# Two groups' inverse deviations at once, and rows normalised four steps behind at the head of ScalarE's step

## The reference

```python
x = _layernorm(x + _L0_gnn_ref(x, ...))   # attention over the edges, 4 heads of 16, then a gate:
    # beta = sigmoid(concat([out, x_r, out - x_r]) @ W_beta)
    # out = beta * x_r + (1.0 - beta) * out;  return out @ W_m2n
x = _layernorm(x + _L1_gnn_ref(x, ...))   # relu(X @ w1 + segment_sum((X @ w2)[src] * ew, dst) + b)

def _layernorm(x, axis=-1, eps=1e-05):
    m = jnp.mean(x, axis=axis, keepdims=True)
    v = jnp.var(x, axis=axis, keepdims=True)
    return (x - m) / jnp.sqrt(v + eps)
```

## Time and profile before

| | |
|---|---|
| median of 3 runs | 1889.04 us (1883.46 to 1889.10) |
| profiled execution | 1893.35 us, its span 1891.7 us |
| edge-and-dense stage | 53 to 711 us of the span |
| scans | 711 to 811.5 us |
| correction, second layer, rows with edges | 811.5 to 1891.7 us |

### The profile page before, as it was taken

One profiled execution on the slowest core, in us unless ns is written; L12 is line 12 of the kernel. 1 busy time (PEld: TensorE's weight loads), 2 busy tenths in 40 slices (PEclk: granted clock), 3 DMA queues, 4 the chain that ended last, 5 costly groups with the idle time before them and its releaser, 6 DMA issues.

```text
span 1891.7 us, 35753 instructions
## 1 busy us (share of the span) xinstructions
PE 1232.4 (65%) x8398; PEld 1070.5 (57%) x8398; DVE 1334.5 (71%) x4876; ACT 1227.0 (65%) x4224; POOL 1061.7 (56%) x1183
## 2 busy tenths in 40 slices
PE   0677777776776760077888887777767766665553
PEld 0666666666666650056766665666656655565552
DVE  2677777777777769977777676888888865545453
ACT  0688888888888890047787776888888862222221
POOL 0555555555555531025555555788878856655565
PEclk9999999999999995589999999999999987777886
DMA  5688888888888879114444444988888842222221
GB/s 167 206 285 293 286 276 280 293 287 280 283 289 290 280 246 302 42 49 146 136 148 132 131 147 134 290 255 256 256 248 260 261 139 74 75 73 73 74 73 40
DMA packets 210063, 371.55 MB, mean 196 GB/s; under 512 B 36724, under 2 KB 67805, under 8 KB 208919
## 3 DMA queue, kind: packets, MB, share of 16 engines
q1 hardware_dynamic: 120822, 200.52, 33.7%
q10 hardware_dynamic: 57739, 108.12, 15.4%
q0 software_dynamic: 31360, 61.17, 13.1%
HBM read 231.39 MB, written 161.37 MB: 208 GB/s over the span
## 4 chain that ended last, share of the span: by engine, by line
PE 24%; issue 21%; POOL 16%; DVE 11%; ACT 10%; another core or an unknown queue 7%; DMA 6%; SPq 4%; ACTq 1%; DVEq 0%; POOLq 0%
POOL ring_a L487 11%; PE pd L552 5%; POOL big L493 4%; PE pk L531 3%; DMA scan_buf<-in_xT 3%; PE pd L583 2%; PE pd L582 2%; DVE val L1043 2%; ACT scan_buf L705 1%; PE pk L652 1%; PE pd L549 1%; ACT hout L705 1%; SPq L322 1%; DMA ew_t<-in_ew 1%
## 5 line engine op out<-in xcount | busy, mean ns | idle before, releaser
L946 DVE BATCH_NORM_STATS2 stats<-hpre 128x6 f32<-128x256 f32 x882 | 334.1, 420 | 0.1
L450 POOL DMA_INDIRECT ring_a<-in_x,gidx x196 | 185.5, 946 | 256.0 <-PE pt L543 208.7
L705 ACT ACTIVATE scan_buf<-hpre,nb,rs 128x128 f32<-128x128 f32 x686 | 292.1, 480 | 22.0 <-issue 13.1
L705 ACT ACTIVATE hout<-hpre,nb,rs 128x128 f32<-128x128 f32 x686 | 292.4, 481 | 20.0 <-issue 12.6
L472 POOL DMA_INDIRECT h_tab<-alpha,sidx x148 | 151.2, 1021 | 214.8 <-ACT alpha L776 169.4
L487 POOL DMA_INDIRECT ring_a<-h_tab,gidx x196 | 209.7, 1070 | 60.1 <-POOL big L493 52.3
L984 DVE SCALAR_TENSOR_TENSOR hpre<-pd,beta,xg 128x128 f32<-128x128 f32 x784 | 220.8, 345 | 25.3
L552 PE MATMUL pd<-w_sx,scan_buf 128*128 128x129 f32 x1568 | 232.8, 278 | 0.0
L531 PE MATMUL pk<-b_kvq,pair 128*128 128x192 f32 x392 | 117.2, 381 | 172.8 <-issue 161.2
L453 POOL DMA_INDIRECT ring_b<-in_x,gidx x196 | 185.4, 946 | 60.5 <-issue 60.5
L552 PEld LDWEIGHTS pd<-w_sx,scan_buf 128*128 128x128 f32 x1568 | 210.6, 194 | 4.8
(11 more groups left out here) (188 smaller groups left out, 3458.3 us busy)
## 6 DMA issues: line engine op xcount, KB each, us to landing
xg<-in_x SPq DMA_DIRECT2D x196, 256.0 KB
scan_buf<-in_xT SPq DMA_DIRECT2D x196, 256.0 KB
val<-h_tab SPq DMA_DIRECT2D x139, 256.0 KB
h_tab<-hout ACTq DMA_DIRECT2D x98, 256.0 KB
h_tab<-scan_buf ACTq DMA_DIRECT2D x98, 256.0 KB
out_z<-hout ACTq DMA_DIRECT2D x98, 256.0 KB
out_z<-scan_buf ACTq DMA_DIRECT2D x98, 256.0 KB
h_two<-h_tab SPq DMA_DIRECT2D x57, 256.0 KB, 8.9
```

Of the source, the lines that this page charges most:

```text
L450: gp.indirect_dma_start(out=ring_a[:, u, :], out_offset=None, in_=x[:, :], in_offset=bass.IndirectOffsetOnAxis(ap=gidx[:, k, 0:1], axis=0))\
L705: ins = act.activation(hout[ju][:, i * D:(i + 1) * D], hpre[:, ju, i * D:(i + 1) * D], ACT.Identity, bias=nb_of(ju, i), scale=rs_of(ju, i))
L946: ins = dve.bn_stats(stats[:, ju, i, :, :].rearrange("p j s -> p (j s)"), two)
```

## The change

Three things change, all in the edge-and-dense stage. ScalarE makes Ln and Exp for two groups at once, in even steps only, for groups k-2 and k-1, behind the gate's Exp. VectorE makes the negated means of two groups at once, in odd steps only, for groups k-3 and k-2, behind its `hpre` instructions. ScalarE normalises all four rows of group k-4 (not k-3) at the head of its step, ahead of the `val` copy. The store of group k-4 stays at the step's end. VectorE's program has one more step at the end.

```diff
--- before.py
+++ after.py
@@ -161,6 +161,9 @@
         def nb_of(ju, i):
             return nb[:, ju, i // 2, i % 2:i % 2 + 1]
 
+        def spread_of(ju, n):
+            return stats[:, ju:ju + n, :, :, :].rearrange("p u a b s -> p (u a b) s")[:, :, 2]
+
         def mean_of(ju, i):
             return stats[:, ju, i // 2, i % 2, 1:2]
 
@@ -709,6 +712,11 @@
             act.wait_ge(S["z_cp"], 16)
 
             def step_a(k, u, it):
+                if live(k, 4, T):
+                    g, gu, itg = back(k, u, it, 4)
+                    wait(act, S["nb_d1"], g + 1)
+                    wait(act, ring["h_st"][gu], 16 * itg)
+                    scale_rows(gu, NJ).then_inc(S["na_d1"], 1)
                 if live(k, 1, T):
                     j, ju, _ = back(k, u, it, 1)
                     wait(act, S["kv_a"], j + 1)
@@ -727,20 +735,15 @@
                     wait(act, S["mm_d1"], k + 1)
                     wait(act, S["pre_d1"], k - 1)
                     exp_minus(act, em[:, u % 2, :], pd[:, u % 2, :, D], S["cl_d1"], S["em_d1"], k)
-                if live(k, 3, T):
-                    g, gu, itg = back(k, u, it, 3)
-                    wait(act, S["nb_d1"], g + 1)
-                    wait(act, ring["h_st"][gu], 16 * itg)
-                    scale_rows(gu, NJ - 1)
-                if live(k, 1, T):
-                    wait(act, S["bn_d1"], j + 1)
-                    act.activation(lv[:, ju, :, :], stats[:, ju, :, :, 2], ACT.Ln, bias=eps_c[:, 0:1], scale=1.0 / D)\
-                        .then_inc(S["lv_d1"], 1)
-                if live(k, 3, T):
-                    scale_rows(gu, NJ, NJ - 1).then_inc(S["na_d1"], 1)
-                if live(k, 1, T):
-                    wait(act, S["lv_d1"], j + 1)
-                    act.activation(rs[:, ju, :, :], lv[:, ju, :, :], ACT.Exp, scale=-0.5).then_inc(S["rs_d1"], 1)
+                if u % 2 == 0 and live(k, 2, T):
+                    g, gu, _ = back(k, u, it, 2)
+                    wait(act, S["bn_d1"], g + 2)
+                    act.activation(lv[:, gu:gu + 2, :, :].rearrange("p u a b -> p (u a b)"), spread_of(gu, 2), ACT.Ln,
+                                   bias=eps_c[:, 0:1], scale=1.0 / D).then_inc(S["lv_d1"], 2)
+                    wait(act, S["lv_d1"], g + 2)
+                    act.activation(rs[:, gu:gu + 2, :, :].rearrange("p u a b -> p (u a b)"),
+                                   lv[:, gu:gu + 2, :, :].rearrange("p u a b -> p (u a b)"), ACT.Exp, scale=-0.5)\
+                        .then_inc(S["rs_d1"], 2)
                 if live(k, 4, T):
                     g, gu, _ = back(k, u, it, 4)
                     wait(act, S["na_d1"], g + 1)
@@ -986,14 +989,18 @@
                             scalar=beta[:, u % 2, i:i + 1], in1=xg[:, u, i * D:(i + 1) * D],
                             op0=ALU.mult, op1=ALU.add)
                     ins.then_inc(S["pre_d1"], 1)
-                if live(k, 2, T):
-                    g, gu, _ = back(k, u, it, 2)
-                    wait(dve, S["rs_d1"], g + 1)
-                    neg_mean(gu, NJ // 2).then_inc(S["nb_d1"], 1)
+                if u % 2 == 1 and live(k, 3, T):
+                    g, gu, _ = back(k, u, it, 3)
+                    wait(dve, S["rs_d1"], g + 2)
+                    dve.scalar_tensor_tensor(
+                        out=nb[:, gu:gu + 2, :, :].rearrange("p u a b -> p (u a b)"),
+                        in0=stats[:, gu:gu + 2, :, :, :].rearrange("p u a b s -> p (u a b) s")[:, :, 1], scalar=-1.0,
+                        in1=rs[:, gu:gu + 2, :, :].rearrange("p u a b -> p (u a b)"),
+                        op0=ALU.mult, op1=ALU.mult).then_inc(S["nb_d1"], 2)
                 if live(k, 0, T):
                     wait(dve, S["pre_d1"], k + 1)
                     pair_stats(u, NJ // 2).then_inc(S["bn_d1"], 1)
-            run_steps(dve, T, 2, step_a)
+            run_steps(dve, T, 3, step_a)
 
 
             dve.wait_ge(S["v_a"], T)
```

## The result

The changed kernel takes 2024.08 us (median of 4 runs, 2021.16 to 2024.39) against 1886.25 us for the kernel before (median of 4, 1882.74 to 1889.10): ratio 1.0726, 95% interval 1.0702 to 1.0750. It is 138 us slower.

A forecast was written before the change was run, and what follows sets the result against it. ScalarE, its instructions and issue time, was taken to bound the stage. A four-step loop of 3.66 + 4.50 + 3.57 + 4.50 = 16.23 us against 13.13 gave about +144 us, so 2033 us, range 2010 to 2075.

The forecast's parts named there:

- Exp to the first row, odd to even: ScalarE's even-step rows wait for VectorE's negated mean from the step before, starting 2.12 us after the gate's Exp starts.
- Four rows: ScalarE's four row instructions at the step's head take 4 x 0.385 = 1.54 us, to the next start.
- `val` to Exp: On ScalarE, from the `val` copy's start to the gate's Exp: 0.84 us, as in a quiet step before.
- Exp to the first row, even to odd: On ScalarE, grouped Ln and Exp, then the store's issue: rows start 1.19 us after the gate's Exp starts.
- 8 numbers cost nothing more than 4: Grouped Ln and Exp on ScalarE handle 8 numbers per partition instead of 4, costing at most 0.01 us more.
- The extra 0.09 us at u = 0: The step after u = 0 stays 0.09 us longer, as before: 3.66 us from Exp to Exp instead of 3.57.
- The drain: One more step at the stage's end adds 2 us: four rows of 1.54 and an issue.
- The waits on loads: 7.5 us of the stage's 647.6 are waits on loads, which a slower loop should mostly absorb; +7 if they stay.
- Rival 1: TensorE's clock falls in its longer idle gaps, Relu of odd steps waits 0.7 us: 2101, or 2067 in half; chance 0.18.
- 1.08 us of cover: TensorE's product ends at 2.20 us after Exp's start; Relu of an odd step asks at 3.28, so it is covered.
- rival 2: Negated mean is there in time and grouping pays: -0.52 us a loop, -25 us, 1864 us; chance 0.04.
- rival 3: The wait is met but the store's issue is bared: 13.72 us a loop, +29 us, 1918; chance 0.04.

The follow-up runs named there:

- second run: The changed kernel run again without edit, in the group of runs where the kernel before takes about 1760 us: 1897.56 us against 1760.06, ratio 1.0779.
- the one with the rows back: Changed kernel with the four rows, still four behind, moved back behind the gate's Exp, ahead of the grouped Ln and Exp: 1824.69 us against 1759.14, ratio 1.0373.
- kernel before with the store moved: Kernel before with the store moved from the step's end to between the `big` copy and Relu: 1723.09 us against 1760.06, ratio 0.9782.
- kernel with the longer wait: Changed kernel with the two groups' negated means made behind the two stats instructions of VectorE's odd step: 1997.59 us against 1759.14, ratio 1.1348.
- kernel with the negated means first: Changed kernel with the two groups' negated means made at the head of VectorE's odd step, ahead of `ep`: 1766.5 us against 1759.14, ratio 1.0040.
- all three together: Changed kernel with negated means ahead of `ep` and the store between `big` and Relu: ratio 0.9800 in one group of runs, 1.0153 in the other.

## Why the prediction was right

**Direction and mechanism.** Forecast 2033 us with 2010 to 2075, measured 2024. The wait came where it was placed: ahead of the rows of even steps, on the negated mean of the step before. Removing it alone takes back 130 of 137.5 us; making it 0.79 us longer costs the 77 us that this predicts, and 24 more in the other steps. The cause is shown, not only argued. The second run's trace names `nb` as what ended the wait in 75 even steps, 1.9 us on average.

**The sum.** Forecast 16.23 us in a loop, measured 15.94; the forecast's +144 became +131 in the span. Its terms:

- Exp to the first row, odd to even: 2.12 forecast; 2.20 (u = 3) and 2.10 (u = 1: 408.33 to 410.43) measured. The negated mean ends 1.77 us behind the Exp, for 1.78 forecast, and the release took 0.13 us at u = 3 where the forecast had 0.04.
- Four rows: 1.54 forecast, 1.55 measured.
- `val` to Exp: 0.84 taken from the earlier trace rows, 0.76 measured (404.06 to 404.82). Four times 0.08 is about the 0.3 us that the loop is shorter; the other errors of this list, +0.12 and -0.09, nearly cancel. This is the term of the sum that was mis-sized. In the kernel before `val`, `q_sb` and `big` start 0.12 and 0.15 us apart, here 0.10 and 0.11. So the spacing was not the instructions' own, as I had taken it to be, and the runs show what it hangs on. `val` to Exp is 0.84 us in the kernels where `val` starts idle, 0.18 us behind the end of the store's issue (both traces of the kernel before, and the one with the rows back). It is 0.76 in those where rows run ahead of `val` and the store stays at the step's end. In the kernel before with the store moved, `val`, `q_sb` and `big` start 0.10 us apart too. The store ahead of `val` was what spread them; why it does is not shown.
- Exp to the first row, even to odd: 1.19 forecast, 1.20 measured, but by luck, since two errors cancel. The store is issued at E + 0.76 and not at E + 0.67, mostly because Exp starts 0.38 behind the Ln of 8 numbers instead of 0.31; and the rows start 0.10 behind the issue's end instead of 0.18. The forecast that 8 numbers cost nothing more than 4 was short by these 0.07 us; the durations of the instructions (0.29 for 0.28) don't show it. The grouped Ln also counts its semaphore up by two and not by one, and no run separates that from the 8 numbers.
- The extra 0.09 us at u = 0: not there (3.51 and 3.50).
- The drain: from the last Exp to the scans 12.8 us instead of 10.3, forecast 2 more.

**The waits on loads** were forecast to be mostly absorbed; the slowest step from odd to even is 4.54 us and only one from even to odd reached 4.0, so they were.

**Rival 1, the clock.** Half right. The granted clock over the stage fell to 0.93 from the 0.98 of the earlier trace rows: between 60 and 830 us it fell to the lower level 32 times, for 3.4 us each, so in about one pair of steps in three. But this stayed hidden, and only just:

```profile
406.88 1.07 PE L555 MATMUL pd<-w_sx,scan_buf 128*128 128x129 f32 x4
...
408.04 0.26 ACT L669 ACTIVATE em<-pd,top_c 128x4 f32<-128x4 f32 x1
```

The rival had TensorE's work at the lower clock throughout, 4.1 us, and Relu 0.7 us late. In the loop the clock fell only ahead of the products: the work from 404.69 to 407.95 took 3.26 us, and Relu started 0.09 us behind it, in its turn. So the 1.08 us of cover was nearly used up in such steps, and Relu waited for TensorE once. The kernel with the longer wait used up the rest, and there it cost some 24 us.

**Rivals 2 and 3** turned on the wait being met, which it wasn't. The kernel with the negated means first is the nearest test of what they would have given: a loop of 13.23 us, between the 12.6 of rival 2 and the 13.72 of rival 3. The grouping's gain is real (42 us in that order of instructions), and the bared store and the bared Ln ate it. The Trainium skill's rule (Trace Analysis, Optimizing Scalar/DVE Operations), that larger operations can help a saturated engine, agrees with that 42 us and not with the change as a whole: under the new wait ScalarE was busy 536 of 770 us (70%) and no longer saturated.

## What to carry to other kernels

When work is moved to the head of an engine's step, look not at how many steps old its inputs are but at what stands between their making and the new place: here a distance of four steps held no cover at all, because the input was made at the end of the step before, behind the very instruction that this engine had just finished. The first repair to try is on the other engine, by making the small value ahead of a wait that it doesn't need; here that took back 130 of 137.5 us. And an issued DMA cost its engine time here only where nothing was queued behind which it could hide. Moving it moves that cost: moved alone, in the kernel before, it gained 2% in one group of runs, where the change with its repair alone was 0.4% slower than the kernel before; with all three together the gain was again 2% there, and 1.5% were lost in the other group. Such a gain has to be measured in both before it is believed.

## What the runs showed of the hardware

- The same program (negated means first, store moved) had ratio 0.980 to the kernel before in one group of runs and 1.015 in the other. The kernel before differed between the groups by some 126 us; of the changed kernel's 126.5 us, 124 are behind the edge-and-dense stage.
- In the slower of these two runs Relu, where it was late, started as much as 3.0 us behind the end of the products it needs; in the other 0.04 us.
- ScalarE's dependent Exp started 0.31 us behind a Ln of 4 numbers per partition, and 0.38 behind one of 8 (medians; the second also counts its semaphore up by two).
- With idle pieces of about 2.2 us ahead of every second burst TensorE's granted clock fell to its lower level in about one such pair of steps in three (2.18 us ahead of 404.69 in the changed kernel, products of 1.02 us from 405.85 on), where the single piece of 2.18 us in the earlier trace rows had left it alone. In the kernel with the negated means last, where TensorE idled about 3 us ahead of most second bursts (2.97 ahead of 516.68), it fell 55 times between 60 and 830 us where the changed kernel had 32, and the stretch's clock was 0.87.
